# A new order of jobs in a fused cross-attention and mixture-of-experts kernel

## The reference

```python
q1 = split_heads(x1 @ Wq1, N1)
k = jnp.concatenate([x1 @ Wk1, x2 @ Wk2], axis=1)   # split in heads
v = jnp.concatenate([x1 @ Wv1, x2 @ Wv2], axis=1)
attn = jax.nn.softmax(einsum('bihd,bjhd->bhij', q1, k) * scale, axis=-1)
x = x + einsum('bhij,bjhd->bihd', attn, v) @ Wo + bo
h = layernorm(x) * gamma + beta
shared_out = silu(h @ q(shared_w1).T) @ q(shared_w2).T
routed_out = top-1 expert of 8 by softmax(h @ router_w.T), times its probability
out = x + shared_out + routed_out
```

## Time and profile before

| | |
|---|---|
| median of 3 runs | 925.86 us (924.48 to 926.16) |
| the profiled execution, its own time | 926.61 us |
| its span in the trace | 924.9 us |
| share of the span that PE, ACT, POOL, DVE are busy | 77%, 75%, 66%, 66% |
| share of the steady batches' time that DMA engines are busy | about 75% |

### The profile page before, as it was taken

One profiled execution on the slowest core, in us unless ns is written; L12 is line 12 of the kernel. 1 busy time (PEld: TensorE's weight loads), 2 busy tenths in 40 slices (PEclk: granted clock), 3 DMA queues, 4 the chain that ended last, 5 costly groups with the idle time before them and its releaser, 6 DMA issues.

```text
span 924.9 us, 22065 instructions
## 1 busy us (share of the span) xinstructions
PE 713.7 (77%) x8022; PEld 495.8 (54%) x8022; DVE 608.8 (66%) x1241; ACT 693.4 (75%) x1536; POOL 614.8 (66%) x669
## 2 busy tenths in 40 slices
PE   2768888897988788898879897889777542788883
PEld 1425656574656565565646564656554421466662
DVE  4457666675666566666657576666664239799994
ACT  5368888988888888979888978888796410588882
POOL 2146686868686867777686868686776723477773
PEclk9779999999999999999999999999998755899997
DMA  6057668686686867677877677686748400244420
GB/s 216 25 133 134 133 125 161 115 154 145 139 164 132 152 120 158 120 161 125 159 119 149 138 144 168 130 149 132 138 93 148 101 3 23 87 124 133 124 74 13
DMA packets 301980, 114.72 MB, mean 124 GB/s; under 512 B 274211, under 2 KB 291117, under 8 KB 301874
## 3 DMA queue, kind: packets, MB, share of 16 engines
q1 hardware_dynamic: 296594, 99.66, 54.9%
q0 software_dynamic: 5280, 13.64, 4.8%
HBM read 35.40 MB, written 13.50 MB: 53 GB/s over the span
## 4 chain that ended last, share of the span: by engine, by line
PE 30%; DVE 25%; POOL 16%; ACT 14%; issue 10%; DMA 4%; DVEq 1%; SPq 0%; ACTq 0%; POOLq 0%
PE FB L327 10%; POOL p_split L509 6%; PE TBK L327 5%; POOL g_lo L531 3%; DMA pt<-p_split 3%; DVE x L1142 3%; PE S L1272 3%; DVE gate L970 2%; DVE pt L1152 2%; DVE ot_lo L955 2%; ACT p_split L699 2%; DVE w_raw L1156 2%; POOL gate L527 2%; ACT k_st L671 2%; ACT th L731 2%
## 5 line engine op out<-in xcount | busy, mean ns | idle before, releaser
L509 POOL TENSOR_TENSOR p_split<-probs,p_split 128x512 f16<-128x512 f32 x256 | 301.7, 1183 | 77.3 <-ACT p_split L699 75.8
L759 ACT ACTIVATE probs<-S,neg_max 128x512 f32<-128x512 f32 x256 | 175.3, 685 | 15.3 <-DVE neg_max L1101 15.3
L1101 DVE TENSOR_REDUCE neg_max<-S 128x1 f32<-128x512 f32 x256 | 171.6, 677 | 8.0 <-PE S L1272 7.9
L699 ACT ACTIVATE p_split<-probs 128x512 f16<-128x512 f32 x256 | 161.2, 630 | 6.7 <-DMA pt<-p_split 1.0
L1288 PE MATMUL O<-v_st,pt 128*128 128x64 f16 x1024 | 120.7, 196 | 54.5 <-DMA pt<-p_split 49.6
L327 PE MATMUL FB<-xt_hi,w_split 128*128 128x256 f16 x768 | 144.1, 277 | 22.9 <-DVE v_st L924 11.5
L1288 PEld LDWEIGHTS O<-v_st,pt 128*128 128x128 f16 x1024 | 92.4, 99 | 120.7 <-DMA pt<-p_split 56.4
L1290 PE MATMUL O<-v_st,pt 128*128 128x64 f16 x1024 | 119.5, 195 | 0.0
L1289 PE MATMUL O<-v_st,pt 128*128 128x64 f16 x1024 | 119.4, 195 | 0.0
L1272 PE MATMUL S<-k_st,q_st 64*128 64x512 f16 x768 | 106.9, 385 | 3.1 <-ACT probs L759 3.1
L327 PE MATMUL FB<-xt_lo,w_split 128*128 128x256 f16 x384 | 106.0, 276 | 0.0
(11 more groups left out here) (230 smaller groups left out, 1928.8 us busy)
## 6 DMA issues: line engine op xcount, KB each, us to landing
rows<-row SPq DMA_DIRECT2D x16, 512.0 KB, 4.3
w_raw<-in_L_ffn_expert_w SPq DMA_DIRECT2D x15, 512.0 KB, 4.2
c_in<-in_ctx SPq DMA_DIRECT2D x16, 256.0 KB, 3.2
x_in<-in_x SPq DMA_DIRECT2D x16, 256.0 KB, 3.7
xb<-in_x SPq DMA_DIRECT2D x16, 256.0 KB, 3.0
pt<-p_split SPq DMA_TRANSPOSE x256, 3.1
k_st<-in_L_xattn_Wk SPq DMA_DIRECT2D x2, 512.0 KB, 8.0
w_split<-rows,p_split POOLq DMA_INDIRECT x39, 3.4
```

The lines of the kernel that those rows point to most:

```text
L509: g.tensor_tensor(p_split[n % HL_RING][:, 1, :], probs[n % PROBS_RING][:, :], p_split[n % HL_RING][:, 0, :], ALU.subtract).then_inc(p_lo_r ...
L699: a_(p_split[g % HL_RING][:, 0, :], probs[g % PROBS_RING][:, :], ACT.Copy).then_inc(p_hi_ready, 1)
L759: a_(probs[g % PROBS_RING][:, :], S[u % 4][:, :], ACT.Exp, bias=neg_max[:, u % 4:u % 4 + 1], accum_out=sums[:, u:u + 1])\
L1101: v.tensor_reduce(neg_max[:, u % 4:u % 4 + 1], S[u % 4][:, :], AX.X, ALU.max, negate=True)\
```

## The change

Five edits, made together:

- `split_probs(n-1)` stands first in POOL's unit in place of last. So it comes ahead of the gate work, of the four small steps of each layer norm, and of the other jobs of that unit.
- The front jobs have another order and other units: `FC_X` moves from unit 5 to 3, right after the unit in which `x1` is made; `Q0`, `K0`, `Q1`, `K1` follow in units 4 to 7, then `V2`, `V3`, `K2` in 8 to 10 and `K3` in 12; unit 11 is free. The waits on `f_lo` and the order in which the weights are loaded at the start follow that.
- In PE's unit the tail job (and `DOWN`) comes after the scores and no longer ahead of them.
- ACT sums an expert matrix in unit 3, no longer in unit 1.
- SP loads the next context in unit 3, no longer in 4.

```diff
-FC_CTX, V2, FC_X, V3, Q0, Q1, K0, K1, K2, K3, V0, QUANT, V1 = range(13)
-FRONT_AT = {2: FC_CTX, 4: V2, 5: FC_X, 6: V3, 7: Q0, 8: Q1, 9: K0, 10: K1, 11: K2, 12: K3, 13: V0, 14: QUANT, 15: V1}
+FC_CTX, FC_X, Q0, K0, Q1, K1, V2, V3, K2, K3, V0, QUANT, V1 = range(13)
+FRONT_AT = {1: FC_CTX, 3: FC_X, 4: Q0, 5: K0, 6: Q1, 7: K1, 8: V2, 9: V3, 10: K2, 12: K3, 13: V0, 14: QUANT, 15: V1}
...
-SUMS_AT = 1
+SUMS_AT = 3
...
@@ GpSimd's body
                 for u in units_of(b):
                     n = b * UNITS + u
+                    if 0 <= n - 1 < NU:
+                        split_probs(n - 1)
                     if has_down(b) and u < 2:
                         gate_rest(b - 2, u)
...
                     if has_tail(b) and u >= 14:
                         gate_scale(t, u - 14)
-                    if 0 <= n - 1 < NU:
-                        split_probs(n - 1)
...
@@ TensorE's front_job
-                elif j in (V2, Q0):
-                    pe.wait_ge(f_lo, f * SPLIT + j)
+                elif j == Q0:
+                    pe.wait_ge(f_lo, f * SPLIT + FC_X + 1)
                 else:
-                    pe.wait_ge(f_lo, f * SPLIT + j - 1)
+                    at_least(pe, f_lo, f * SPLIT + j - 1)
...
@@ TensorE's body
+                    if has_front(b) and u in FRONT_AT:
+                        front_job(b, par, FRONT_AT[u])
+                    if u % 4 == 0 and 0 <= g - LAG < NU:
+                        weigh_values(g - LAG)
+                    if u % 2 == 0 and 0 <= g + 2 < NU:
+                        scores(g + 2)
                     if has_down(b) and u == DOWN_AT:
                         tail_job(b - 1, DOWN)
-                    if has_front(b) and u in FRONT_AT:
-                        front_job(b, par, FRONT_AT[u])
                     if has_tail(b) and u in TAIL_AT:
                         tail_job(b, TAIL_AT[u])
...
-                    if u % 4 == 0 and 0 <= g - LAG < NU:
-                        weigh_values(g - LAG)
-                    if u % 2 == 0 and 0 <= g + 2 < NU:
-                        scores(g + 2)
```

More of the change, by code:

```diff
@@ L47 @@
 ABSENT = 8192
-FC_CTX, V2, FC_X, V3, Q0, Q1, K0, K1, K2, K3, V0, QUANT, V1 = range(13)
-FRONT_AT = {2: FC_CTX, 4: V2, 5: FC_X, 6: V3, 7: Q0, 8: Q1, 9: K0, 10: K1, 11: K2, 12: K3, 13: V0, 14: QUANT, 15: V1}
+FC_CTX, FC_X, Q0, K0, Q1, K1, V2, V3, K2, K3, V0, QUANT, V1 = range(13)
+FRONT_AT = {1: FC_CTX, 3: FC_X, 4: Q0, 5: K0, 6: Q1, 7: K1, 8: V2, 9: V3, 10: K2, 12: K3, 13: V0, 14: QUANT, 15: V1}
 FRONT = 13
+K_JOBS = (K0, K1, K2, K3)
 SPLIT = 12
@@ L95, in xattn_ffn @@
         minus_half = sb("minus_half", [P, TB], F32)
-        WV2, WQ, WK1, WK2, WV1 = range(5)
+        WQ, WK1, WK2, WV2, WV1 = range(5)
         w_split = sb("w_split", [P, 2, 5, DC, INNER], F16)
@@ L414, in _ @@
             sp.dma_start(x_in[:, :, :], x_v[0]).then_inc(x_loaded, 16)
-            for n, w in ((WV2, wv2), (WQ, wq1), (WK1, wk1), (WK2, wk2), (WV1, wv1)):
+            for n, w in ((WQ, wq1), (WK1, wk1), (WK2, wk2), (WV2, wv2), (WV1, wv1)):
                 sp.dma_start(landing[n].rearrange("p (c n) -> p c n", c=DC),
@@ L447, in body @@
                     if has_front(b) and f + 1 < B:
-                        if u == 4:
+                        if u == 3:
                             sp.wait_ge(f_full, f * FRONT + FC_CTX + 1)
@@ L667, in front_hi @@
                 elif j in (Q0, Q1):
-                    s = 2 * (j - Q0)
+                    s = 2 * int(j == Q1)
                     a_(q_st[:, fp, 0, s:s + 2, :], fb2[k], ACT.Copy, scale=1.0 / WSCALE).then_inc(f_hi, 1)
                 else:
-                    a_(k_st[fp][:, 0, j - K0, :], FB[k][:, :], ACT.Copy, scale=1.0 / WSCALE).then_inc(f_hi, 1)
+                    a_(k_st[fp][:, 0, K_JOBS.index(j), :], FB[k][:, :], ACT.Copy, scale=1.0 / WSCALE).then_inc(f_hi, 1)
             def normalise(dst, src, rs, shift, done):
@@ L926, in front_lo @@
                 elif j in (Q0, Q1):
-                    s = j - Q0
+                    s = int(j == Q1)
                     v.scalar_tensor_tensor(q_st[:, fp, 1, 2 * s:2 * s + 2, :], fb2[k], 1.0 / WSCALE,
@@ L930, in front_lo @@
                 else:
-                    c = j - K0
+                    c = K_JOBS.index(j)
                     v.scalar_tensor_tensor(k_st[fp][:, 1, c, :], FB[k][:, :], 1.0 / WSCALE, k_st[fp][:, 0, c, :],
@@ L1221, in front_job @@
                 k = (j + fp) % 2
-                if is_static(f) and f == 0 and j in (V2, Q0, K0, V0):
-                    pe.wait_ge(w_lo_ready, {V2: 1, Q0: 2, K0: 4, V0: 5}[j])
+                if f == 0 and j in (Q0, K0, V2, V0):
+                    pe.wait_ge(w_lo_ready, {Q0: 1, K0: 3, V2: 4, V0: 5}[j])
                 if j == FC_CTX:
@@ L1246, in front_job @@
                     for n in range(2):
-                        cols = slice((2 * (j - Q0) + n) * P, (2 * (j - Q0) + n + 1) * P)
+                        c0 = 2 * int(j == Q1) + n
+                        cols = slice(c0 * P, (c0 + 1) * P)
                         last = split_product(fb2[k][:, n, :], [(w_hi[:, WQ, c, cols], w_lo[:, WQ, c, cols],
@@ L1252, in front_job @@
                 else:
-                    cols = slice((j - K0) * P, (j - K0 + 1) * P)
+                    c0 = K_JOBS.index(j)
+                    cols = slice(c0 * P, (c0 + 1) * P)
                     for n, w in enumerate((WK1, WK2)):
@@ L1264, in scores @@
                 if ib == 0:
-                    pe.wait_ge(f_lo, b * SPLIT + K0 + c + 1)
+                    pe.wait_ge(f_lo, b * SPLIT + K_JOBS[c] + 1)
                 if g >= 4:
```

## The result

The changed kernel takes 1041.49 us (median of four runs, 1038.02 to 1045.40) against 925.42 us (924.48 to 926.16) before: the ratio is 1.126, 95% interval 1.121 to 1.130. It is slower, as forecast, but by 116 us and not by 76, and the time lies above the range. The profiled execution took 1041.13 us.

The account below looks back on a forecast made before the run. The prediction took the order in which PE and ACT hand work to each other as the bound. 926.6 + 42.7 (parts one to three) + 13.7 (part four) + 21 (clock) - 2 (batch 15) = 1002 us, range 945 to 1030.

Parts of the forecast that it names:

- the walk: Step-by-step timing of one steady batch of the changed kernel through all four engines: period 47.05 us, 4.1 more than before.
- time 0: End of the token normalisation, when PE can start `FC_X`; the walk through a batch starts and ends there.
- walk, without the clock: The walked batch before the clock's 1.5 us is added: a period of 47.05 us against 42.96 before.
- First and second part: Time 0 to `Q0` (start 5.25 us), then to the tail's norm (22.3): 4.5 us lost, 1.6 sums, 2.9 waits.
- The clock: PE's 4.1 us wait ahead of `Q0` halves its clock: 1.5 us a batch (1.1 to 4.2), 21 us in all.
- The third part: From the tail norm's start to the second tanh's end: 13.45 us against 14.94 before, 1.5 us gained.
- The fourth part: Second tanh's end back to time 0: ACT waits 2.5 us for `shift`, 1.05 us lost, 13.7 us over 13.
- Start and end: Kernel start: 0 us (bounds -2 and 3); batch 15, without a front: 2 us back (bounds 0 and 3.7).
- The clock stays up: Rival: PE's clock does not fall, so 21 us fall away: 982 us, chance 0.25.
- Only the sums are paid: Rival: ACT takes up the rest in slack, leaving 14 x 1.6 = 22 us: 949 us, chance 0.12.
- Faster: Rival: only PE's waits for transposed probabilities change, 2.4 us a batch and 3.7 in batch 15: 888 us, chance 0.10.
- The signs that the prediction named: Period some 48.5 us; waits: `xt_lo` about 4, `K0` 3 to 4, `shift` 2.5, none for `pt`; clock 0.50 behind `xt_lo`.

Follow-up runs that it names:

- changed, both gaps filled: Changed kernel plus useless matmuls on PE, 56 ahead of `Q0` and 48 behind `K3`, sums in unit 3: ratio 1.080, period 48.03 us on average.
- changed, second gap filled: Changed kernel plus 48 useless matmuls on PE behind `K3` only: ratio 1.104, period 49.5 us.
- changed, first gap filled: Changed kernel plus 56 useless matmuls on PE ahead of `Q0` only: ratio 1.092, period 49.5 us.
- the fillers: Useless matmuls, 56 ahead of `Q0` and 48 behind `K3`, added to the changed kernel: ratio 1.080, or 1.079 with the sums in unit 1.
- the last experiment: Kernel before with the subtraction first in POOL's units 13 to 15, `FC_X` in unit 3 and `V2` in unit 5: ratio 0.997.

## Why the prediction was right in its direction and wrong in its size

The stretches of the walk, as means over the batches between 240 and 720 us of each trace (nine or ten each). Each stretch ends where the walk ended it: start of the norm of the tail, start of the second tanh and 0.72, end of the next normalisation.

| us | to the norm | to the second tanh | to time 0 | sum |
|---|---|---|---|---|
| before | 17.8 | 14.9 | 10.3 | 43.0 |
| walk, without the clock | 22.3 | 13.45 | 11.3 | 47.05 |
| changed, both gaps filled | 22.1 | 14.8 | 11.15 | 48.0 |
| changed, second gap filled | 23.8 | 14.8 | 11.15 | 49.7 |
| changed, first gap filled | 22.1 | 16.25 | 11.15 | 49.5 |
| changed | 23.65 | 16.4 | 11.15 | 51.2 |

- **First and second part, held.** `Q0` starts at 459.79, 4.88 us after time 0, where the walk had 5.25; the norm comes at 22.1 at full clock (22.3). But the walk's account of it was wrong in one place: it gave 1.6 us to the sums, and the kernel without them there is only 0.65 to 1.0 us faster in this stretch, which it loses again in the fourth. The tail jobs behind the scores, which the walk did not price by themselves, cost 1.75 us a batch alone (in the batches of 44.7 us, 1.2 of it in this stretch, 18.9 against 17.7, and 0.6 in the next). With the sums priced too high by 0.6 us or more and the total right to 0.2, other waits must have been priced too low: that the total came out is in part luck.
- **The clock, held as far as it went.** 1.5 us for the fall ahead of `Q0`; measured 23.65 less 22.1. The Trainium skill (TensorE: Matmul & The Clock Gate, Part 1) has the clock halved after an idle stretch, and the traces with and without fillers agree. But the reason given, that 4.1 us is longer than the waits behind which the clock fell, does not hold: here it fell in the first 0.4 us of the stand of 3.58 us, and in the trace before it also fell after shorter waits. One of them stands just ahead of the batch of the earlier trace rows, whose clock the prediction took to have stayed up:

```profile
392.88 0.23 PE L1288 MATMUL O<-v_st,pt 128*128 128x64 f16 x1 [2.15 <-DMA pt<-p_split]
```

```profile
392.00:394.00 2.00, 1.12 (x15) 1.00 (x16) 1.24 (x4) 2.00 (x7) 2.00 (x2) 0.65 0.55 108
```

  That clock was back at about 396.0, as the next normalisation began, and the batch took its usual 42.9 us; the one at 307 us lasted until 310.8, into the jobs behind the normalisation, and cost 1.1. What a fall costs thus hangs on what PE has to do in it.
- **The third part failed.** "ACT comes to the end of the second tanh at 35.75, 13.45 us after the norm's start [...] 1.5 us gained". It takes 16.4, 2.95 more. At full clock 1.3 us of that are missing (14.8): the gain of 1.5 us never came. The walk had no stand of PE there. But the value product of unit 12 may not start before DVE has emptied the bank `O` into `o_sb`, and DVE comes to that only behind the low half of `K2` (which itself waits 0.97 us for ACT) and a maximum. The same eviction in the kernel before, and PE's `K3` there:

```profile
421.56 0.42 DVE L942 TENSOR_TENSOR o_sb<-O,inv_sum 128x256 f32<-128x256 f32 x1
```

```profile
420.89 0.28 PE L327 MATMUL FB<-xt_hi,w_split 128*128 128x256 f16 x1 [0.75 <-DVE k_st L932]
```

  and in the changed kernel with both gaps filled, with its norm and its second tanh:

```profile
462.19 0.42 DVE L943 TENSOR_TENSOR o_sb<-O,inv_sum 128x256 f32<-128x256 f32 x1
```

```profile
455.27 1.09 ACT L676 ACTIVATE row<-x,shift,rs 128x256 f32<-128x256 f32 x2 [0.98 <-POOL shift L576]
...
469.31 0.84 ACT L732 ACTIVATE th<-TBK,half_up 128x256 f32<-128x256 f32 x2
```

  The eviction starts 6.93 us after the norm's start before (414.63), 6.92 in the changed kernel (485.32 less 478.40) and 6.92 with the gaps filled. The new table does not touch what leads up to it on ACT and DVE. Before, PE did `K3` in this time; now `K3` is done by 482.7 and PE stands for 3.04 us. From the eviction to the second tanh it is 7.29 us before, 7.12 with the gaps filled and 8.79 in the changed kernel: these 1.65 us are the second fall of the clock. Over 14 batches 2.95 us make 41, and the miss is 1041 - 1002 = 39.
- **The fourth part, held.** ACT waits 2.3 us for `shift` (predicted 2.5), and the stretch takes 11.15 us (11.3). The subtraction alone costs more in the kernel before, 11.9 against 10.3 us, since the sums still stand in unit 1 there.
- **Start and end.** The start was right (0.3 us). Batch 15 was to give 2 us back. What follows the last normalisation is 6.7 us longer; parts one to three cost 7.3 there as elsewhere, so at most 0.6 came back.
- **Rivals.** "The clock stays up" is, ahead of `Q0` and behind `K3`, what the fillers made: 999.55 us with the sums in unit 1, a ratio of 1.08 with them in either unit, where I had worked out 982; the 17 us between are the third part again, 14 times 1.3. "Only the sums are paid" is refuted, since they are the one thing that costs next to nothing. "Faster" would have needed the waits for `pt` to be worth their length. They went, and the new ones are longer together (9.5 us of PE in the batch shown, against 2.4).

The signs that the prediction named came true: a wait of 3.6 us for `xt_lo`, 2.3 for `shift`, 2.9 for `K0`, a clock of 0.50 ahead of `Q0`, none for `pt`. Only the period was off, and no sign looked at the third part. That DVE's eviction of `O` holds this part at its old length is read from three traces; no run moved the eviction, so how much of the 1.3 us would come back without it stays open.

## What to carry to other kernels

Where engines work in a fixed order, a job that is moved is also a job that others are moved past: the subtraction was wanted earlier by PE's value products and later by everything that POOL does for ACT, and moving it only in the three units where nothing critical stood behind it was the version that won (0.987). Walk the whole period when a table of jobs changes, also the units that become empty, and look there for stands of PE above all, since one with critical work of PE behind it can be paid a second time by the clock. Ask of each job that is moved forward what it waits for at its new place, and whether that has moved too: `K3` came earlier, the emptying of `O` did not. When the clock falls in some batches and not in others, hold it up with useless matmuls first and compare single parts then.

## What was not expected of the hardware

- The clock fell behind stands shorter than those that the prediction drew on (3.64 us): behind 3.04 us in unit 12, behind 2.39 us in most batches of the last experiment, and in the kernel before at a stand of 2.15 us. The same stand of 2.39 us in neighbouring batches left the clock at 1.00 once and took it to 0.50 the other time, for 1.26 us of the period.
- One kernel has several steady rhythms. With the sums in unit 1 the changed kernel alternates between 49.6 and 52.8 us, and with the tail jobs ahead of the scores it changes within one execution from some 48.6 to 49.7 us a batch to 51.1 to 51.4, and its runs lie up to 45 us apart.
- About a hundred extra matmuls of 128 columns a batch (PE busy 43.14 us in place of 39.17) made the kernel 4% faster (999.55 us and a ratio of 1.079 with the sums in unit 1, against 1041.49 us and 1.126).
